# Summing K times V over tokens: from one-column matmuls to the diagonal of a 128x128 matmul

## What is computed

```
QKV = X @ W_in.T + b_in;  Q, K, V = split(QKV)
Q, K = rope(Q), rope(K)             # first 128 of 256 features, in pairs
A = sum over tokens of (K / max(|K|, 1e-12)) * V      # 256 numbers
Y = (A * Q) @ W_out.T + b_out
x = layernorm(x + Y + x)
```

## Time and profile before

| | us |
|---|---|
| median of 3 runs | 152.6 (152.34 to 152.65) |
| span of the profiled execution | 150.5 |
| what lies around the span, against the median | 2.1 |
| PE busy | 135.8 (90%) |
| DVE busy | 105.7 (70%) |
| ACT busy | 77.3 (51%) |
| POOL busy | 67.6 (45%) |

### The profile page before, as it was taken

One profiled execution on the slowest core, in us unless ns is written; L12 is line 12 of the kernel. 1 busy time (PEld: TensorE's weight loads), 2 busy tenths in 40 slices (PEclk: granted clock), 3 DMA queues, 4 the chain that ended last, 5 costly groups with the idle time before them and its releaser, 6 DMA issues.

```text
span 150.5 us, 2427 instructions
## 1 busy us (share of the span) xinstructions
PE 135.8 (90%) x802; PEld 118.9 (79%) x802; DVE 105.7 (70%) x233; ACT 77.3 (51%) x146; POOL 67.6 (45%) x81
## 2 busy tenths in 40 slices
PE   4999979955999899999999999999999999999920
PEld 4778859825987579897898998998998998989910
DVE  0549899996598938899955965745965654638991
ACT  4515966017076894168064264264265265297571
POOL 3004899913999807048306606707507606000310
PEclk9999997555599999999999999999999999999996
DMA  4899940000003130004000400400300000000034
GB/s 133 213 321 419 387 185 4 0 0 0 2 4 121 44 119 0 0 0 139 4 0 0 139 4 2 139 0 0 139 0 0 0 0 0 4 0 0 0 121 158
DMA packets 4698, 10.55 MB, mean 70 GB/s; under 512 B 545, under 2 KB 2641, under 8 KB 4433
## 3 DMA queue, kind: packets, MB, share of 16 engines
q1 hardware_dynamic: 4688, 10.43, 20.1%
HBM read 9.38 MB, written 1.05 MB: 69 GB/s over the span
## 4 chain that ended last, share of the span: by engine, by line
PE 64%; DVE 20%; DMA 5%; ACT 3%; SPq 3%; issue 1%; ACTq 0%; DVEq 0%
PE ps L878 21%; PE ps L879 20%; PE ps L880 20%; DMA wq<-in_w_q_t 5%; DVE z L607 4%; DVE qa L648 2%; DVE kv L588 2%; SPq L257 2%; DVE x L727 2%; DVE z L678 1%; ACT gT_lo L425 1%; DVE stats L849 1%; DVE fT_lo L699 1%; DVE qb L656 1%; DVE acc L752 1%
## 5 line engine op out<-in xcount | busy, mean ns | idle before, releaser
L738 DVE TENSOR_TENSOR gT_lo<-kv,gT_hi 128x512 fp32r<-128x512 f32 x30 | 26.1, 884 | 26.1 <-ACT gT_hi L509 26.0
L352 POOL TENSOR_TENSOR w_hi<-wraw,zero 128x512 fp32r<-128x512 f32 x16 | 18.9, 1181 | 41.2 <-PE ps L880 41.2
L878 PE MATMUL ps<-w_hi,gT_hi 128*128 128x256 f32 x120 | 33.7, 281 | 0.1
L880 PE MATMUL ps<-w_hi,gT_lo 128*128 128x256 f32 x120 | 33.4, 279 | 0.0
L879 PE MATMUL ps<-w_lo,gT_hi 128*128 128x256 f32 x120 | 33.4, 278 | 0.0
L878 PE MATMUL ps<-fT_hi,w_hi 128*128 128x512 f32 x64 | 25.5, 399 | 0.3 <-DVE fT_lo L699 0.3
L879 PE MATMUL ps<-fT_lo,w_hi 128*128 128x512 f32 x64 | 25.4, 396 | 0.0
L880 PE MATMUL ps<-fT_hi,w_lo 128*128 128x512 f32 x64 | 25.3, 395 | 0.0
L507 ACT ACTIVATE kv<-ps,b_now 128x512 f32<-128x512 f32 x16 | 11.0, 690 | 24.7 <-PE ps L880 24.5
L878 PEld LDWEIGHTS ps<-w_hi,gT_hi 128*128 128x128 f32 x120 | 22.7, 189 | 1.1 <-issue 0.4
L752 DVE SCALAR_TENSOR_TENSOR acc<-ps,comb,acc 128x256 f32<-128x256 f32 x53 | 22.6, 475 | 1.0 <-PE ps L880 0.7
(11 more groups left out here) (139 smaller groups left out, 243.1 us busy)
## 6 DMA issues: line engine op xcount, KB each, us to landing
wraw<-in_expert_w SPq DMA_DIRECT2D x8, 512.0 KB, 3.4
xT<-in_x_t SPq DMA_DIRECT2D x4, 256.0 KB, 5.6
acc<-in_x_tok SPq DMA_DIRECT2D x1, 1024.0 KB, 9.5
rT<-in_rope_t SPq DMA_DIRECT2D x1, 1024.0 KB, 10.8
out<-z SPq DMA_DIRECT2D x4, 256.0 KB, 2.2
wkv<-in_w_kv_t SPq DMA_DIRECT2D x2, 256.0 KB, 3.6
rtok<-in_rope_tok SPq DMA_DIRECT2D x1, 512.0 KB, 7.8
brow<-in_b_rows SPq DMA_DIRECT2D x1, 384.0 KB, 6.4
```

What stands on the lines that cost most here:

```text
L352: g.tensor_tensor(w_hi[:, slot, cols], src, zero[:].to_broadcast([P, 2 * D]), ALU.add).then_inc(w_part, 1)
L738: v.tensor_tensor(low, h[:, i, :], raw(high), ALU.subtract).then_inc(g_lo_ok, 1)
L878: nc.tensor.matmul(dst, lh, rh, start=k == 0, stop=False)
L880: last = nc.tensor.matmul(dst, ll, rh, start=False, stop=k == len(terms) - 1)
```

## The change

K times V is no longer made elementwise. ACT multiplies V by `krec` (a per-token scale) into `z`, and PE multiplies K, as stationary operand, by scaled V, 128 features by 128 features for each block, over all eight tiles. The wanted sums stand on the diagonal of the 128x128 result. DVE multiplies it by the identity and sums the rows into `acol`, one instruction for each block. The rotation goes by pairs of tiles: POOL has (0,1), (2,3) and (4,5), DVE has (6,7). The feature sum is in one piece, ahead of both Q blocks of half 1. ACT's doublings, its second half of Q and POOL's residual and `other(1)` take new places in their orders.

```diff
-        POOL_ROTATES = ((0, 2), (2, 3), (4, 6), (6, 7))
-        DVE_ROTATES = (3, 7)
+        POOL_ROTATES = ((0, 2), (2, 4), (4, 6))
+        DVE_ROTATES = (6, 8)
...
             other(0)
             q_pass_low(0)
-            pool.wait_ge(q_pass_lo_ok, 1)
-            other(1)
             pool.wait_ge(l_brow, 16)
             residual(0, TPH)
+            pool.wait_ge(q_pass_lo_ok, 1)
+            pool.wait_ge(res_ok, 1)
+            other(1)
             q_pass_low(1)
...
+            def v_scaled(t):
+
+                act.wait_ge(krec_ok, t // TPH + 1)
+                a.activation(z[:, t, :], kv[:, t, D:2 * D], ACT.Copy, scale=krec[:, t:t + 1]).then_inc(vs_ok, 1)
...
+            for t in range(TPH):
+                k_square(t)
+            k_norm(0)
+            k_square(4)
+            k_square(5)
+            v_scaled(0)
+            v_scaled(1)
+            k_square(6)
+            v_scaled(2)
+            v_scaled(3)
+            k_square(7)
+            k_norm(1)
...
             q_raw(0)
+            for t in range(TPH, T):
+                v_scaled(t)
+            twice(0)
             q_pass(0)
+            q_rot_high(0)
+
+            act.wait_ge(l_wout, 16)
+            for k in range(KD):
+                act.wait_ge(acol_ok, k + 1)
+                a.activation(wo_hi[:, k, :], wout[:, k, :], ACT.Copy, scale=acol[:, k:k + 1]).then_inc(wo_hi_ok, 1)
             q_raw(1)
-            q_rot_high(0)
-
-            act.wait_ge(l_wout, 16)
-            act.wait_ge(acol_ok, 1)
-            for k in range(KD):
-                a.activation(wo_hi[:, k, :], wout[:, k, :], ACT.Copy, scale=acol[:, k:k + 1]).then_inc(wo_hi_ok, 1)
             q_pass(1)
+            twice(1)
             q_rot_high(1)
...
             kv_out(2)
             kv_out(3)
-            dve.wait_ge(l_rtok, 16)
-            rotate(3)
             kv_out(4)
             dve.wait_ge(wq_hi_ok, 1)
             v.tensor_tensor(wq_lo[:], wq[:], raw(wq_hi[:]), ALU.subtract).then_inc(wq_lo_ok, 1)
-            kv_product(0)
             kv_out(5)
-            kv_product(1)
-            kv_product(2)
+            k_reciprocal(0)
             kv_out(6)
-            kv_product(3)
-            k_reciprocal(0)
             kv_out(7)
-            rotate(7)
+            dve.wait_ge(kv_ok, T)
+            rotate(*DVE_ROTATES)
             k_reciprocal(1)
-            for t in range(4, T):
-                kv_product(t)
...
             q_products(0)
             q_rotate(0)
-            q_products(1)
+            dve.wait_ge(a_mm, 1)
             for k in range(KD):
+                v.scalar_tensor_tensor(out=diag[:, k, :], in0=ps[:, 2 + k, 0:P], scalar=1.0, in1=ident[:],
+                                       op0=ALU.mult, op1=ALU.mult, accum_out=acol[:, k:k + 1]).then_inc(acol_ok, 1)
+            dve.wait_ge(q_hi_ok, 2)
+            v.tensor_tensor(gT_lo[:, 0, half(0)], qT[:, 0, half(0)], raw(gT_hi[:, 0, half(0)]),
+                            ALU.subtract).then_inc(q_rot_lo0_ok, 1)
+            for k in range(KD):
+                dve.wait_ge(acol_ok, k + 1)
                 dve.wait_ge(wo_hi_ok, k + 1)
                 v.scalar_tensor_tensor(out=wo_lo[:, k, :], ...)
+            q_products(1)
             q_rotate(1)
...
+            def feature_sum(t):
+
+                pe.wait_ge(vs_ok, t + 1)
+                if t < DVE_ROTATES[0]:
+                    pe.wait_ge(rot_ok, t // 2 + 1)
+                else:
+                    pe.wait_ge(vrot_ok, 1)
+                for k in range(KD):
+                    last = nc.tensor.matmul(ps[:, 2 + k, 0:P], kv[:, t, tile(k)], z[:, t, tile(k)],
+                                            start=t == 0, stop=t == T - 1)
                 return last
...
             pe.wait_ge(kv_ok, T)
-            feature_sum(0)
+            for t in range(T):
+                last = feature_sum(t)
+            last.then_inc(a_mm, 1)
             q_block(1, 0)
-            feature_sum(1).then_inc(a_mm, 1)
             q_block(1, 1)
```

More of the change, by code:

```diff
@@ L95, in layer_kernel @@
         acol = sb("acol", [P, KD])
+        diag = sb("diag", [P, KD, P])
         wo_hi = sb("wo_hi", [P, KD, D], F32R)
@@ L164, in layer_kernel @@
             sem(n) for n in "wkv_hi_ok wkv_lo_ok xT_hi_ok xT_lo_ok wq_hi_ok wq_lo_ok".split())
-        kv_mm, kv_ok, rot_parts, rot_ok, vrot_parts, vrot_ok, kv_prod, ksq_ok, knorm_ok, kfloor_ok, krec_ok = (
-            sem(n) for n in "kv_mm kv_ok rot_parts rot_ok vrot_parts vrot_ok kv_prod ksq_ok knorm_ok kfloor_ok krec_ok".split())
+        kv_mm, kv_ok, rot_parts, rot_ok, vrot_parts, vrot_ok, vs_ok, ksq_ok, knorm_ok, kfloor_ok, krec_ok = (
+            sem(n) for n in "kv_mm kv_ok rot_parts rot_ok vrot_parts vrot_ok vs_ok ksq_ok knorm_ok kfloor_ok krec_ok".split())
         q_mm, q_raw_ok, qab_ok, q_other_ok, q_rot_ok, q_pass_ok, q_hi_ok, q_rot_lo0_ok, q_rot_lo1_ok, q_pass_lo_ok = (
@@ L419, in _, with k_square @@
             a.copy(wq_hi[:], wq[:]).then_inc(wq_hi_ok, 1)
-            for t in range(T):
+            def k_square(t):
                 act.wait_ge(kv_ok, t + 1)
@@ L426, in _, with k_norm, twice @@
                              accum_out=ksq[:, t:t + 1]).then_inc(ksq_ok, 1)
[L427 to L435, removed]
+            def k_norm(n):
+                act.wait_ge(ksq_ok, (n + 1) * TPH)
+                q4 = slice(n * TPH, (n + 1) * TPH)
+                a.activation(knorm[:, q4], ksq[:, q4], ACT.Sqrt).then_inc(knorm_ok, 1)
+            def v_scaled(t):
+                act.wait_ge(krec_ok, t // TPH + 1)
+                a.activation(z[:, t, :], kv[:, t, D:2 * D], ACT.Copy, scale=krec[:, t:t + 1]).then_inc(vs_ok, 1)
+            def twice(n):
+                act.wait_ge(l_x, 16)
+                four = slice(n * TPH, (n + 1) * TPH)
+                a.mul(acc[:, four, :], acc[:, four, :], 2.0).then_inc(res_dbl, 1)
+            for t in range(TPH):
[10 more added lines that the diff above has]
+            k_norm(1)
             act.wait_ge(l_cols, 16)
@@ L457, in _ @@
             q_raw(0)
+            for t in range(TPH, T):
+                v_scaled(t)
+            twice(0)
             q_pass(0)
-            q_raw(1)
             q_rot_high(0)
             act.wait_ge(l_wout, 16)
-            act.wait_ge(acol_ok, 1)
             for k in range(KD):
+                act.wait_ge(acol_ok, k + 1)
                 a.activation(wo_hi[:, k, :], wout[:, k, :], ACT.Copy, scale=acol[:, k:k + 1]).then_inc(wo_hi_ok, 1)
+            q_raw(1)
             q_pass(1)
+            twice(1)
             q_rot_high(1)
@@ L588, in kv_out, with rotate @@
                 v.tensor_tensor(kv[:, t, :], ps[:, t % 4, :], bkv, ALU.add).then_inc(kv_ok, 1)
-            def rotate(t):
-                i = DVE_ROTATES.index(t)
-                dve.wait_ge(kv_ok, t + 1)
+            def rotate(t0, t1):
+                dve.wait_ge(l_rtok, 16)
                 for c in range(2):
[L595 to L607, removed]
+                    v.tensor_tensor(*rotary_product(t0, t1, 0, c), ALU.mult)
+                    v.tensor_tensor(*rotary_product(t0, t1, 1, c), ALU.mult).then_inc(vrot_parts, 1)
+                dve.wait_ge(vrot_parts, 2)
+                dve.wait_ge(ksq_ok, t1)
+                v.tensor_tensor(*rotary_sum(t0, t1, 0), ALU.subtract)
+                v.tensor_tensor(*rotary_sum(t0, t1, 1), ALU.add).then_inc(vrot_ok, 1)
             def k_reciprocal(n):
@@ L648, in q_products @@
                 v.tensor_tensor(qa[:, n, :], qT[:, 0, half(n)], rT[:, 0, half(n)], ALU.mult).then_inc(qab_ok, 1)
[L649 to L655, removed]
                 v.tensor_tensor(*other_product(n, ODD, EVEN), ALU.mult).then_inc(qab_ok, 1)
@@ L911, in q_block @@
                     .then_inc(q_mm, 1)
[L913 to L917, removed]
-                    for k in range(KD):
-                        last = nc.tensor.matmul(ps[:, 2 + k, 0:1], z[:, t, tile(k)], krec[:, t:t + 1],
-                                                start=t == 0, stop=t == T - 1)
+            def feature_sum(t):
[7 more added lines that the diff above has]
+                                            start=t == 0, stop=t == T - 1)
                 return last
```

## The result

The change makes the kernel 1.5% faster: 150.02 us median (148.66 to 151.47, 11 runs) against 152.17 us for the kernel before (11 runs). The ratio is 0.9846, 95% interval 0.9812 to 0.9880, so 2.3 us were won; 2.8 were forecast.

What follows compares the result with a forecast made beforehand. VectorE's turns lost to GpSimd were taken to delay PE's output projection, at 35.62 us. It would start at 32.15 or 33.55, gaining 3.5 or 2.1, middle 2.8: 152.6 - 2.8 = 149.8 us, own range 148.6 to 151.0, overall 147.0 to 152.0.

Steps and rivals of the forecast that it cites:

- What binds: Before the experts: two-SBUF-operand VectorE instructions wait for GpSimd's running instruction; four products took 4.66 us, `qa` 2.85 us.
- The stall is moved, not removed: Ahead of the output projection: GpSimd's residual (2.42 us), which cost `qa` its time, now costs `wo_lo`.
- Rival B: VectorE gets in ahead of the residual, PE starts near 28.6 to 30.0 us, gaining 5.5 to 6.9: 146.4; chance 0.10.
- The date to follow: PE's start on the output projection, 35.62 us before the change; its shift was taken as the gain, 2.8 us.
- The start of the projection: PE's first output-projection matmul: 32.15 us in the early case, 33.55 us in the late case, against 35.62 before.
- Early or late: Two cases for the column norm's reciprocals, 22.3 or 23.7 us; gain 3.5 or 2.1 us, middle 2.8 taken.
- the sixth either slips in or waits behind `other(0)`: VectorE's rotation of tiles 6 and 7: sixth instruction at 21.8 us, or 23.2 behind GpSimd's `other(0)`; trace undecided.
- 0.3 us to spare: Second half of q: GpSimd's low part ready at 37.0 us, just ahead of tile 4 at 37.3 us.
- Rival C: The second half binds: one more GpSimd turn of 1.3 us on the late case leaves 0.8, so 151.8 us; chance 0.15.
- No gain is booked: VectorE's last normalisations, 2.33 us for two, may meet GpSimd again though residuals and weight splits come 0.3 to 1.4 earlier.
- Rival A: Clock stays at 1.2 GHz past 46 us after PE's idle gap: 2.5 us slower, 155.1; chance 0.11.
- The rule against the rows: SBUF port rule would also block GpSimd's residual and `other(1)`: gain 1.6 us, 151.0, instead of 2.8 by the rows.

Runs made afterwards that it cites:

- The hold in the kernel before: Kernel before, with GpSimd's part of q held until the eight K-V products are done and the first residual until q of half 0 is rotated: 151.63 us, ratio 0.9991.
- GpSimd held: Kernel after, with GpSimd's first residual add held until both wo_lo parts are done: 150.09 us median, ratio to before 0.9857.
- PE kept busy: Kernel after, with 15 plain float32 identity matmuls into a free PSUM bank where PE idles ahead of the output projection: 148.74 us, ratio 0.9806.
- the run that fills GpSimd's idle time: Kernel after, doubling and q_pass(0) moved into ScalarE's idle time, first residual held until q half 0 is rotated, other(1) until wo_lo is done: 148.10 us, ratio 0.9755.
- the profiles with 21.5 and 21.7 us: Second reciprocal's end in two changed kernels after: matmuls filling PE's idle time (21.46; 148.74 us) and first residual held until wo_lo is done (21.72; 150.09 us).

## Why the prediction was right

- *What binds.* Right: VectorE's turns against GpSimd. The hold in the kernel before shows it (4.66 to 1.42 us for the products). "The stall is moved, not removed" holds as well (3.97 us at `wo_lo`, 0.87 when held). Rival B, no turns lost, fell with those rows.
- *The date to follow.* Wrong for the kernel after. "PE's start on the output projection at 35.62 us is therefore the date to follow" held before the change. After it the chain runs over VectorE alone from `wo_lo` to the first sum at 35.69 us, since `qa` and `qb` of half 1 moved behind `wo_lo`. The projection could start 3.1 us earlier without gain (GpSimd held), and tiles 0 to 3 could run 1.5 us faster without gain (PE kept busy). That a shift of 2.93 us in this date went with a gain of 2.3 us is in part luck, since the gain came by another chain.
- *The start of the projection.* 32.15 or 33.55 was forecast, 32.69 came. The last `kv` was done at 19.0 (19.1 forecast), the feature sum ended near 25.5 (25.1 or 26.2), `diag` took 0.29 us (0.3), a 128x128 float32 matmul 4.0/16 = 0.25 us (0.256), and the scaled copies 1.71 us for four (1.8).
- *Early or late.* The step "the sixth either slips in or waits behind `other(0)`" had the right place. In the kernel after the rotation got through, and the floor of 4 columns behind it lost the turn, 1.23 us; in the run that fills GpSimd's idle time it was a rotation, as written, 1.38 us. Both cases exist; the profiles with 21.5 and 21.7 us are the early ones, 0.6 to 0.8 us earlier than the 22.3 forecast, as GpSimd's rotations ended by 21.0 to 21.3 us and not at 21.45. In the kernel after it came at 22.8 us rather than 23.7, since only the second reciprocal was left to do behind `other(0)`, and that ended at 22.6.
- *Tile 4.* "0.3 us to spare" was too much: GpSimd's low part was 0.52 us late. PE needed 4.6 us for tiles 0 to 3, partly at full clock, where 5.1 was reckoned (24 times 6.08/28 would be 5.2), and the low part came 5.1 us after PE's start, not 4.85. Rival C's place was right, its price was not: the 0.52 us did not take from the gain, since VectorE was not waiting for PE.
- *The term that was off.* "No gain is booked" for the last normalisations, so no loss either; but the turns there were worse than before: 1.7 us more on three `shift` instructions, of which 0.3 came back at the normalisations. I read this from rows; no run took GpSimd's weight splits away. Tile 3's sum came 3.6 us earlier instead of my 2.8. So one miss of 0.8 us and one of 1.4 us in the other direction partly cancelled and left 2.2, and the total is closer to the forecast than its parts.
- *The clock.* Rival A did not occur: the clock fell after the idle gap, as feared, but was back near 37 us, some 4 us after the restart. Its price for the first experts never came up.
- *The rule against the rows.* By the Trainium skill, "SBUF — State Buffer", section "Who interferes with whom", whichever of the two issues second is blocked for the whole instruction of the other, GpSimd too. The rows bear it out in part: the residual took 2.79 us here against 2.42 before, and `other(1)` 1.52 to 1.70 in kernels where VectorE was ready first, while in the kernel after it took 1.27. GpSimd lost 0.2 to 0.4 us in a turn, less than the 0.44 to 0.69 us of the VectorE instruction, and VectorE 1.0 to 2.2 us. The start of the projection came 2.93 us earlier, nearer to the 2.8 by the rows than to the 1.6 by the rule.

## What to carry to other kernels

When VectorE and GpSimd both read SBUF, count GpSimd's instructions as time taken from VectorE's two-operand instructions (here each cost 0.2 to 0.7 us less than its own length), and ask of a change whether it lowers that sum or only moves it. What helped here was to take work off VectorE altogether (to ScalarE and to a matmul whose diagonal is read from PSUM, about 2 us against the same orders with the old sum) and to put GpSimd's work where VectorE would wait (2.1 us by the profiles, 0.7 to 1.4 by the ratios). A hold on GpSimd is cheap to try, but look at the next two-operand instructions before counting the gain, and follow the chain of waits again after the change: the date that bound before need not be the one that binds now.

## What was not expected of the hardware

- An instruction of 4 columns with one SBUF operand and a constant (the floor) loses a turn as an instruction of 512 does: 1.23 us instead of 0.16.
- A plain float32 matmul of 128x128 with one moving column and one with 128 cost the same: 1.95 us for eight of either kind at full clock (sixteen records each). The row of the new form is above (ps<-z,kv); that of the old one, from TensorE's timeline of the kernel before:

```profile
21.84 1.95 PE L919 MATMUL ps<-krec,z 128*128 128x1 f32 x16 [0.87 <-DVE kv L588]
```

- Keeping PE busy through an idle stretch did not remove the dip of the clock. It began 15.0 us after the reciprocal instead of 10.8, behind the next idle time, of 2.00 us, and in work that had run at full clock before.
